# An attention pass whose first twelve pairs of row tiles, instead of eight, are gathered ahead of it

## The reference, cut to what matters

```python
h = (x @ W.T).reshape(n, 8, 64)
e = leaky_relu(e_src + e_dst, 0.2) * (1.0 + et_emb[edge_type]) * edge_weight[:, None]
e_max = zeros((n, 8)).at[dst].max(e)
e = exp(e - e_max[dst])
e_sum = zeros((n, 8)).at[dst].add(e)
msg = h[src] * (e / (e_sum[dst] + 1e-10))[:, :, None]
out = zeros((n, 8, 64)).at[dst].add(msg).reshape(n, 512) + x
```

## Time and profile before

| what | us |
|---|---|
| median of three runs | 1908.78 |
| the profiled execution | 1905.63 |
| its span | 1903.9 |
| first instruction of the pass (ACT, L718) | at 1105.07 |
| first and last gather in the pass (POOL, L688) | at 1112.99 and 1311.79 |
| last matmul of the pass (PE, L784) | at 1324.48 |

### The profile page before, as it was taken

How to read it: one execution, slowest core, us unless ns; L and a number is a source line. 1 busy time by engine, 2 the same in 40 slices (tenths; PEclk the granted TensorE clock), 3 DMA queues, 4 the chain that set the end, 5 groups by cost and what they waited for, 6 DMA issues and landing times. The chain is left out here.

```text
span 1903.9 us, 26664 instructions
## 1 busy us (share of the span) xinstructions
PE 1596.2 (84%) x7565; PEld 956.2 (50%) x7566; DVE 1161.4 (61%) x2308; ACT 459.8 (24%) x875; POOL 700.1 (37%) x605
## 2 busy tenths in 40 slices
PE   6556939876698999998788379996698899999998
PEld 6524723335344555554555245553346445864486
DVE  7889959974375777775577766665865722122222
ACT  3101114424013555553344110000110111001100
POOL 0005878874475766640000547775330110000000
PEclk9988969998698999999799589999799999999999
DMA  0056841009315666680496447776005202330033
GB/s 26 1 215 247 286 118 12 3 2 358 133 39 155 209 188 187 187 143 34 176 361 236 133 121 210 210 209 158 2 1 173 70 0 106 138 111 0 1 138 137
DMA packets 76360, 249.16 MB, mean 131 GB/s; under 512 B 14901, under 2 KB 28582, under 8 KB 68346
## 3 DMA queue, kind: packets, MB, share of 16 engines
q1 hardware_dynamic: 38618, 147.08, 21.2%
q0 software_dynamic: 34592, 96.87, 19.0%
q10 hardware_dynamic: 3072, 4.20, 0.8%
HBM read 215.93 MB, written 32.00 MB: 130 GB/s over the span
## 5 line engine op out<-in xcount | busy, mean ns | idle before, releaser
L659 POOL DMA_INDIRECT tab_slots<-slot_words,slot_address x160 | 232.4, 1452 | 219.7 <-issue 209.0
L688 POOL DMA_INDIRECT e_rows<-tab_h,idx_h x176 | 178.7, 1015 | 290.5 <-POOLq L50 217.3
L1431 PE MATMUL dense_pY<-weights,dense_xT_block 128*128 128x512 f32 x640 | 284.0, 601 | 0.0
L1479 PE MATMUL dense_pY<-parts,dense_number 128*128 128x512 f32 x1000 | 237.2, 398 | 5.7 <-DMA dense_number<-tab_edges_to 5.7
L982 POOL DMA_INDIRECT e_rows<-tab_q,idx_q x192 | 182.0, 948 | 99.8 <-PE e_pS L1055 38.8
L1479 PEld LDWEIGHTS dense_pY<-parts,dense_number 128*128 128x128 f32 x1000 | 188.3, 189 | 53.3 <-DMA dense_number<-tab_edges_to 6.4
L782 PE MATMUL e_pS<-e_rows,e_onehot_ring 128*128 128x512 f32 x352 | 193.8, 641 | 21.7 <-DVE e_rows L758 18.6
L1431 PEld LDWEIGHTS dense_pY<-weights,dense_xT_block 128*128 128x128 f32 x640 | 121.5, 193 | 143.3 <-issue 143.3
L1055 PE MATMUL e_pS<-e_rows,e_onehot_f 128*128 128x512 f32 x384 | 181.6, 596 | 0.0
L867 PE MATMUL count_pA<-count_onehot_d,count_onehot_s 128*128 128x512 f16 (+1 forms) x576 | 132.4, 352 | 42.0 <-DVE count_onehot_d L850 40.9
L758 DVE TENSOR_TENSOR e_rows<-e_rows,e_pW 128x1024 f32<-128x1024 f32 x88 | 107.3, 1220 | 68.6 <-DMA e_rows<-tab_h,idx_h 68.5
(11 more groups left out here) (310 smaller groups left out, 2393.5 us busy)
## 6 DMA issues: line engine op xcount, KB each, us to landing
basis_piece<-in_L_gnn_basis_pieces SPq DMA_DIRECT2D x32, 2048.0 KB, 7.5
dense_number<-tab_edges_from SPq DMA_DIRECT2D x20, 1280.0 KB, 5.4
tab_edges_from<-counts_turned SPq DMA_DIRECT2D x10, 1280.0 KB
tab_edges_to<-counts_total SPq DMA_DIRECT2D x10, 640.0 KB
dense_number<-tab_edges_to SPq DMA_DIRECT2D x10, 640.0 KB, 4.3
tab_w<-basis_wout ACTq DMA_DIRECT2D x128, 32.0 KB
weights<-tab_w SPq DMA_DIRECT2D x4, 1024.0 KB, 6.3
weights<-in_L_gnn_W_T SPq DMA_DIRECT2D x3, 1024.0 KB
```

Of the source, the lines that this page charges most:

```text
L659: pool.indirect_dma_start(self.table, bass.IndirectOffsetOnAxis(self.address[:, t:t + 1], 0), self.words[:, t, :], None).then_inc(self.pla ...
L688: pool.indirect_dma_start(self.rows[:, q, s, :], None, self.table, bass.IndirectOffsetOnAxis(self.idx[:, j * 2 + s:j * 2 + s + 1], 0)).the ...
L1431: ins = self.nc.tensor.matmul(self.banks.at(g), self.xt[:, b % 2, c, :], weights[:, c, :], start=c == 0, stop=c == 3)
L1479: ins = self.nc.tensor.matmul(self.banks.at(self.first + b), self.number[:, b % 2, r * NB + k, :], self.parts[r][n][:, k, :], start=k == 0 ...
```

## The change

Twelve pairs are gathered in `attention_weights`, the pass starts at pair 12. The four additional places are the tile `vec` (8 vectors of 512 numbers, four pairs of rows), used once, for pairs 8 to 11. The seven vectors that lived there are no longer loaded in the load stage; SyncE loads them in the pass, once pair 11 is summed. Pairs 12 to 15 take ring slots 4 to 7, pairs 16 to 19 slots 0 to 3, and from there on pair j takes slot j mod 8 as before; since slots 0 to 3 are used one time fewer, their counts in `wait_rows` are lower by one. `wait_free` makes GpSimd wait for pair j - 8, and for j - 16 where j is 16 to 19. TensorE and VectorE write out two steps of eight pairs before their loops.

```diff
-def lagged(eng, steps, width, works, last=0):
+def lagged(eng, steps, width, works, last=0, first=1):
...
-    peeled(eng, steps, step, first=1 + most // width, last=last)
+    peeled(eng, steps, step, first=max(first, 1 + most // width), last=last)
...
 class RowRing:
...
-    def __init__(self, nc, ctx, name, table, idx):
+    MORE = 4
+    AHEAD = BODYP + MORE
+
+    def __init__(self, nc, ctx, name, table, idx, room):
...
+        self.more = room.rearrange("p (j s) d -> p j s d", s=2)
         self.got = [sem(f"got{q}") for q in range(BODYP)]
+        self.got_more = [sem(f"got_more{q}") for q in range(self.MORE)]
+
+    def in_more(self, i, u):
+        return isinstance(i, int) and i == 1 and u < self.MORE
+
+    def rows(self, i, u):
+        return self.more[:, u, :, :] if self.in_more(i, u) else self.ring[:, u, :, :]
+
+    def wait_rows(self, eng, i, u):
+        if self.in_more(i, u):
+            eng.wait_ge(self.got_more[u], 32)
+        elif u < self.MORE and not is_first(i):
+            eng.wait_ge(self.got[u], i * 32)
+        else:
+            eng.wait_ge(self.got[u], (i + 1) * 32)
+
+    def wait_free(self, pool, j, summed):
+        before = j - BODYP if j % BODYP >= self.MORE or j >= 3 * BODYP else j - 2 * BODYP
+        pool.wait_ge(summed, before + 2)
...
         @block.gpsimd
         def _(pool):
-            for j in range(BODYP, PAIRS):
-                pool.wait_ge(summed, j + 2 - BODYP)
+            for j in range(ring.AHEAD, PAIRS):
+                ring.wait_free(pool, j, summed)
                 ring.gather(pool, j)
+
+        @block.sync
+        def _(sp):
+            sp.wait_ge(summed, ring.AHEAD + 1)
+            for tile, source in later:
+                sp.dma_start(tile, source).then_inc(later_in, 16)
...
-            lagged(v, NSTEP, BODYP, [(0, build), (0, multiply)])
+            lagged(v, NSTEP, BODYP, [(0, build), (0, multiply)], first=2)
...
-            peeled(pe, NSTEP, step)
+            peeled(pe, NSTEP, step, 2)
...
-            for j in range(BODYP):
+            for j in range(ring.AHEAD):
                 ring.gather(pool, j)
...
                 sp.dma_start(vec[:, 0, :], ins[VECS[0]].partition_broadcast(P)).then_inc(bias_in, 16)
-                for k in range(1, len(VECS)):
-                    sp.dma_start(vec[:, k, :], ins[VECS[k]].partition_broadcast(P)).then_inc(vecs_in, 16)
                 sp.wait_ge(bias_in, 16)
...
-        ring = RowRing(nc, until_dense, "e1", tab["h"], idx["h"])
+        ring = RowRing(nc, until_dense, "e1", tab["h"], idx["h"], vec[:, :, :])
...
-                       side)
+                       side, [(vec[:, k, :], ins[VECS[k]].partition_broadcast(P)) for k in range(1, len(VECS))], vecs_in)
```

More of the change, by code:

```diff
@@ L676, with attention_pass @@
 class RowRing:
-    def __init__(self, nc, ctx, name, table, idx):
+    MORE = 4
+    AHEAD = BODYP + MORE
+    def __init__(self, nc, ctx, name, table, idx, room):
         self.nc, self.table, self.idx = nc, table, idx
         sem = stage_semaphores(nc, ctx, name)
-        self.rows = ctx.enter_context(nc.sbuf_tensor(f"{name}_rows", [P, BODYP, 2, D], F32))
+        self.ring = ctx.enter_context(nc.sbuf_tensor(f"{name}_rows", [P, BODYP, 2, D], F32))
+        self.more = room.rearrange("p (j s) d -> p j s d", s=2)
         self.got = [sem(f"got{q}") for q in range(BODYP)]
+        self.got_more = [sem(f"got_more{q}") for q in range(self.MORE)]
[13 more added lines that the diff above has]
+        pool.wait_ge(summed, before + 2)
     def gather(self, pool, j):
-        q = j % BODYP
+        i, u = j // BODYP, j % BODYP
+        got = self.got_more[u] if self.in_more(i, u) else self.got[u]
         for s in range(2):
-            pool.indirect_dma_start(self.rows[:, q, s, :], None, self.table,
+            pool.indirect_dma_start(self.rows(i, u)[:, s, :], None, self.table,
                                     bass.IndirectOffsetOnAxis(self.idx[:, j * 2 + s:j * 2 + s + 1], 0)
-                                    ).then_inc(self.got[q], 16)
-def attention_pass(nc, name, C, ring, loc, block_turn, block_bank, block_end, acc, weight, side):
+                                    ).then_inc(got, 16)
+def attention_pass(nc, name, C, ring, loc, block_turn, block_bank, block_end, acc, weight, side, later, later_in):
     ns = H + 1
@@ L699, in attention_pass @@
         sem = stage_semaphores(nc, ctx, name)
-        rows, got = ring.rows, ring.got
         ohr = sb("onehot_ring", [P, 4, 2, P], F32)
@@ L755, in multiply @@
             def multiply(i, u):
-                v.wait_ge(got[u], (i + 1) * 32)
-                r = rows[:, u, :, :].rearrange("p s (h d) -> p s h d", h=H)
+                ring.wait_rows(v, i, u)
+                r = ring.rows(i, u).rearrange("p s (h d) -> p s h d", h=H)
                 nc.vector.tensor_tensor(
@@ L781, in step @@
                     for s in range(2):
-                        nc.tensor.matmul(flat(pS[:, bass.ds(bank[u], 1), :]), ohr[:, u % 4, s, :], rows[:, u, s, :],
+                        nc.tensor.matmul(flat(pS[:, bass.ds(bank[u], 1), :]), ohr[:, u % 4, s, :], ring.rows(i, u)[:, s, :],
                                          start=False, stop=True, skip_group_check=True)
```

## The result

The changed kernel takes 1913.57 us (median of 15 runs; the kernel before 1908.78, also 15). The ratio is 1.0032, 95% interval 1.0023 to 1.0041; timed once more on another occasion it is 1.0035 (1.0023 to 1.0046). So the change costs 4 to 9 us, some 6, where the prediction said +1.1, no change, in a range of 1906 to 1913. Three executions lie far above all others and are left out of every ratio and median here: 2694.83 and 3191.60 us of two of the experiments' kernels, and 7231.95 us of the kernel before.

A forecast was written before the change was run, and what follows sets the result against it. GpSimd's issue of gathers, 2.50 us a pair, was taken to set the pass's end. -10.0 + 8.66 + 2.7 - 0.3 = +1.1 us gave 1906.7 by the profiled execution, 1909.8 by the median; range 1906 to 1913.

The forecast's parts named there:

- Eight gathers fewer: In the pass: four pairs move ahead of it, so GpSimd's stream is 8 x 1.250 = 10.0 us shorter.
- The stream starts later: At the pass's start: the first gather, pair 12, waits for pair 4 instead of pair 0, +8.66 us.
- The eight gathers ahead of the pass: Before the pass: GpSimd reaches the barrier at 1107.1, not 1104.4, so the pass starts 2.7 us later; bounds 0 and 4.5.
- The vectors' load: In the pass: seven 256 KB transfers meet the gathers; cost between 0 and 6.2 us, taken as 0.
- Loads taken out of the load stage: In the earlier load stage: seven issues fewer, -0.3 us taken, bounds 0 and -1.1.
- Peeled steps: In the pass: one more step written out on TensorE and VectorE, taken as 0.
- the free barrier: Rival, before the pass: GpSimd gets through earlier or nobody waits, -1.6 us in all, 1907.1; chance 0.14.
- VectorE was not held: Rival, before the pass: a gather holds VectorE and delays the subtraction by 0.75 us, +1.9 in all, 1910.6; chance 0.08.
- The full worth: Rival, in the pass: pair 12 is released early, the 8.66 us is not paid, -7.6 us, 1901.1; chance 0.08.
- The prediction's tail: At the pass's end: last rows land, are multiplied and summed; last matmuls 12.69 us behind the last gather's start.

The follow-up runs named there:

- twelve places written out: Changed kernel with nine pairs gathered ahead, twelve places used in turn up to pair 35, all eleven steps written out: median 1903.18 us, ratio 0.9984.

## Why the prediction was wrong, point by point

- *Eight gathers fewer:* right. 152 gathers ran in the pass at 1.25 us.
- *The stream starts later:* right in kind. After the change pairs 0 and 4 were summed 8.65 us apart in one execution, 9.75 us in the other. The 8.66 us was read from one start of the clock and taken as fixed.
- *The eight gathers ahead of the pass:* this step failed. The working of the eight durations was right, to the tenth. Wrong was "GpSimd takes part in each barrier, so the pass starts 1107.1 - 1104.4 = 2.7 us later": it took the end of the last gather's instruction for GpSimd's arrival. The block's DRAIN waits for the landing, 2.8 us after that end, and ends 1.0 us behind it, so 2.8 + 1.0 = 3.8 us are missing: +6.5 in place of +2.7. Its upper bound, 4.5, was built on instruction ends too, and so did not hold either. The runs show this by taking the gathers away (44.61), by halving them (46.00) and by landing them late (54.43).
- *The vectors' load:* right, nothing. DMA at 292 GB/s, GpSimd's pace unchanged; the landings, up to 8.1 us after the start, were worked off while TensorE was full, as the prediction said.
- *Loads taken out of the load stage:* -0.7 by two executions each (14.2 against 14.7 and 15.2), within the bounds, over the -0.3 taken. All eight executions without these loads, 14.15 to 14.74, have a mean of 14.36, which makes it -0.55.
- *Peeled steps:* right, no cost in the pass by the same runs.
- *Rivals:* the free barrier was the wrong way round: it cost more than the forecast, not less. VectorE was not held: the subtraction at 1097.69 took 2.29 us as before, with a gather let in between the scan and it. The full worth needed another order of the places, and then came: a pass 9.6 us shorter (211.85 against 221.48).

With the one term put right the sum is -10.0 + 8.66 + 6.5 - 0.3 = +4.9 us. By the four executions the three stages give +6.5 - 1.1 - 0.7 = +4.7, ratio 1.0025, inside both intervals but at their lower end. Another 1 to 2 us may lie in the stages behind (dense +1.0 by the same executions); no run settles that, since these scatter as much. The part that is shown is the stage before the pass.

## What to carry to other kernels

When work is moved ahead of a barrier, ask when the engine leaves its block, not when its last instruction ends: with GpSimd's gathers that was here their landing and a microsecond. A longer lead is worth what its first wait allows: with twelve places but pair 12 behind pair 4, nearly the whole gain went into that wait. Cross the barrier with only so many gathers as land in its shadow, and issue the rest first thing behind it.

## What the runs showed that was not expected

- GpSimd's DRAIN at the end of the stage before the pass ended 0.8 to 1.0 us after its last indirect DMA had landed, in five kernels and with landings of 3.7 to 7.0 us; SyncE's DRAIN after two loads of 1 MB took 0.13 us. The time behind the landing is no constant of the engine: at the pass's own end, before, the DRAIN ended near 1323.3, 2.4 us after VectorE had the last rows, and with twelve places written out 4.5 us after. Why is open; nothing waited for it there.

```profile
1320.97 1.22 DVE L758 TENSOR_TENSOR e_rows<-e_rows,e_pW 128x1024 f32<-128x1024 f32 x1 [1.47 <-DMA e_rows<-tab_h,idx_h]
```

```profile
L696 POOLq DRAIN  x1: 23930/23930/23930, 1299.4 to 1299.4; - x1
```

- The last rows of the pass land late in every version: VectorE has them 9.2 us after the start of the last gather (1311.79, 1320.97), 8.9 us in the changed kernel, where it is 3.7 us in the middle of the pass. The prediction's tail holds this unseen; no run shows the cause.
- The time at which TensorE's clock rises in the pass differs between executions of one program (pair 4 summed after 16.1 or 17.6 us), and a stream that waits for an early pair inherits it: 219.71 and 221.54 us.
- 1.8 MB of loads beside the gathers raised DMA from 207 to 292 GB/s and the time to landing to as much as 8.1 us, without lengthening one gather's issue.
